# Attention stages: weighted values and row sums from one matrix product, sums merged and inverted on VectorE, another order of the steps

## Chip, cores and metric

The program runs on 1 core of one Trainium2 chip, as a single program of six stages one after the other. The metric is the device time in microseconds of one execution (the median of several). TensorE (PE) multiplies, VectorE (DVE), ScalarE (ACT) and GpSimd (POOL) work on the elements, SyncE (SP) starts most transfers.

## What is computed

A decoder of two layers on x of shape (16, 256, 256): 16 batches of 256 rows with 256 features, all float32. After each part the input is added and every row normalized to mean 0 and variance 1.

- stage "self": causal self-attention with 32 query heads of 16 features and grouped keys and values. Pairs of heads are subtracted with a learned factor (differential attention), and a second product with the output weights follows.
- stage "cross": attention of 16 heads on a context, without a mask, no biases on queries and keys.
- a mixture of experts, and a state-space layer.
- stage "causal": attention of 16 heads on the context with biases and, as the kernel runs it, a causal mask.
- a feed-forward layer with two chosen low-rank experts.

In each attention, for every head:

```python
s = q @ k.T / sqrt(16)            # masked above the diagonal where causal
p = exp(s - max(s))
o = (p @ v) / sum(p)
y = concat(o) @ Wo                # then x + y, normalized by rows
```

## The kernel before

The kernel is written with an explicit program for each engine, and semaphores between them. Each attention stage is one function: `self_attention` for "self", and `cross_attention` for "cross" and "causal". Each has a `body(st)` per engine, run once per step; a step handles several batches at different points of a pipeline. `st.has(d)` asks whether batch (step + d) exists, and `d` = 3 is the batch whose x is being turned and projected, 2 the one whose stacks are loaded from DRAM, 1 the one whose row maxima are computed, 0 and -1 the ones in exponential and weighted sum, -2 the one in the output product (in "self": 0 and -1). Inside a step a loop runs over pairs of heads, 16 in "self" and 8 in the others; here they are called blocks. The order in which the `if i == ...` lines stand in each engine's loop is the order of that engine's queue, and each engine carries it out strictly. The order is written by hand.

In one block PE does, in this order: `scores` of a pair (L1187 in self, L530 in the others) into `score_ps`, of which there is one; `max_scores` of a pair of the next batch (L1168, L509) into one of two `max_ps` banks, with the causal mask added by `mask_half` (L88); in every fourth block `transpose_max` (L1150, L490) of four pairs' maxima; in every odd block `weighted` (L1212, L555); and in most even blocks a projection or output product into the single bank `misc` (L79 to L81, three products of high and low parts for one float32 product).

The values of two heads of a pair lie side by side in `v_pad`, each padded with 16 zero columns, so that a product with 32 columns gives one head's rows of 16 and adds zero to the other's. `weighted` runs four parts: two (`k` = 0, 1) with `v_pad` into the first 256 columns of `out_ps`, and two with the constant `ones` (`lasting_ones`) into the other 256 columns, which so hold the sum of the probabilities, once for each of the 16 feature rows. `par` is the head of the pair; both heads of a tile collect in the same bank. It begins a new tile once `comb_ready` says that ACT's `keep_weighted` (L1293, L647) has copied the bank to `comb`. DVE's `normalize` takes the reciprocal of the sums (L1430, L739) and multiplies (L1434, L743), for each tile. GpSimd's `part_o` splits the result into high and low parts for the output product.

`take_max` on DVE reduces a pair's scores to row maxima: one instruction in cross (L730), two in the causal stages (L1422 and L1423, L726 and L727), because the score blocks of a causal pair lie at columns 0 to 127 and 256 to 511. ACT copies the transposed maxima (`keep_max`), and one block later its `load_row` writes them by DMA into a row of the query stack (L1266, L630), for which `scores` of that tile waits. Other steps that the change touches: `transpose_x` and the split of x into `x_hi` (ACT) and `x_lo` (DVE, L778) in block 5 of cross and causal; `norm_rows` in block 3, which adds the residual and takes the moments; in self `sort_k` (POOL, L1532) in block 15, `sort_q` of tile 0 (ACT, L1276) in block 14, `output_1` of 24 products in block 14, `pad_v` in block 10.

## Time and profile before

| | |
|---|---|
| median of 3 runs | 2752.08 us (2749.12 to 2754.55) |
| profiled execution, its own time | 2760.98 us |
| its span | 2759.3 us |
| PE / DVE / POOL / ACT busy | 88% / 70% / 56% / 52% of the span |
| instructions | 67851 |
| stage self, first to last scores | 66.6 to 688 us |
| stage cross | 753 to 1079 us |
| stage causal | 2177 to 2490 us |

The busy shares are means over six stages that have different limits, so the windows of single batches are of more use than the page's total. In a timeline a line gives the start in us, the duration in us, the engine, the line of the kernel, the instruction and its tiles, and a count where equal instructions were merged. Records of PE overlap, since matmuls are pipelined: what counts is the distance of the starts.

### The profile page before, as it was taken

The page shows a single profiled execution, that of the slowest core. Times are in us where ns is not written, and L with a number is a line of the kernel's source. Part 1 is how long each engine was busy: PE and PEld are TensorE (multiplying, and loading weights), DVE is VectorE, ACT ScalarE, POOL GpSimd, SP SyncE. Part 2 cuts the span into 40 slices and gives each one's busy share as a digit, 9 for nine tenths or more (in the row PEclk, how much of TensorE's full clock was granted, in tenths as well). Part 3 has the DMA queues.
Part 4 walks back from the last instruction along what each step waited for, and adds up shares of the span by engine and source line. Part 5 has one row for each costly group of instructions (what it writes and reads, how often), then busy time and mean ns, then how long its engine had stood idle before and what let it go on. Part 6 is the DMA issues. An engine that isn't in the chain of part 4 may idle for free. (4 is left out here: it accounts for less than half of the span.)

```text
span 2759.3 us, 67851 instructions
## 1 busy us (share of the span) xinstructions
PE 2433.1 (88%) x25528; PEld 2026.7 (73%) x25528; DVE 1932.2 (70%) x3095; ACT 1434.9 (52%) x2255; POOL 1558.9 (56%) x1873
## 2 busy tenths in 40 slices
PE   5999999998699996998999994888896799997998
PEld 4677667766566764988999993677775577765998
DVE  2677667777377876344888885999985377775776
ACT  2566556655256664323665663656563355553333
POOL 3666566665344542055666665777755477763433
PEclk9899999999699998899999997999997899998999
DMA  8555556651677772024666663111001877851111
GB/s 201 129 148 151 131 145 152 146 131 37 180 185 195 198 202 72 16 96 149 220 229 221 216 217 118 37 41 47 22 13 31 238 192 210 214 140 35 58 57 50
DMA packets 228043, 363.58 MB, mean 132 GB/s; under 512 B 52720, under 2 KB 157168, under 8 KB 220272
## 3 DMA queue, kind: packets, MB, share of 16 engines
q1 hardware_dynamic: 207248, 281.31, 38.8%
q0 software_dynamic: 17376, 78.13, 8.1%
q8 instruction: 157, 2.57, 0.4%
q10 hardware_dynamic: 3200, 1.05, 0.2%
q14 instruction: 62, 0.51, 0.1%
HBM read 231.72 MB, written 133.69 MB: 132 GB/s over the span
## 5 line engine op out<-in xcount | busy, mean ns | idle before, releaser
L1285 ACT ACTIVATE self_probs<-self_score_ps 128x768 f32<-128x768 f32 x256 | 208.1, 813 | 201.2 <-PE self_score_ps L1187 199.2
L1501 POOL TENSOR_SCALAR_AFFINE_SELECT self_probs<-self_probs 128x512 f32<-128x512 f32 x256 | 167.3, 655 | 199.1 <-ACT self_probs L1285 198.7
L1422 DVE TENSOR_REDUCE self_neg_max<-self_max_ps 128x2 f32<-128x256 f32 x256 | 107.9, 422 | 204.0 <-PE self_max_ps L88 203.8
L730 DVE TENSOR_REDUCE cross_neg_max<-cross_max_ps 128x4 f32<-128x1024 f32 x128 | 156.0, 1222 | 77.6 <-PE cross_max_ps L509 76.6
L640 ACT ACTIVATE cross_probs<-cross_score_ps 128x1024 f32<-128x1024 f32 x128 | 131.1, 1024 | 96.7 <-PE cross_score_ps L530 96.5
L1423 DVE TENSOR_REDUCE self_neg_max<-self_max_ps 128x2 f32<-128x512 f32 x256 | 174.2, 681 | 0.0
L2213 POOL TENSOR_TENSOR moee_h_lo<-moee_h,moee_h_hi 128x512 fp32r<-128x512 f32 x78 | 112.0, 1437 | 92.9 <-ACT moee_h_hi L1950 92.1
L1950 ACT ACTIVATE moee_h_hi<-moee_h 128x512 fp32r<-128x512 f32 x110 | 69.5, 632 | 182.0 <-DVE moee_h L2116 152.4
L3508 POOL TENSOR_TENSOR ffn_g_lo<-ffn_g_full,ffn_g_hi 128x512 fp32r<-128x512 f32 x64 | 82.2, 1284 | 129.0 <-ACT ffn_g_hi L3394 116.7
L640 ACT ACTIVATE causal_probs<-causal_score_ps 128x768 f32<-128x768 f32 x128 | 103.8, 811 | 95.4 <-PE causal_score_ps L530 95.3
L1187 PE MATMUL self_score_ps<-self_q_stack,self_k_stack 49*128 49x128 f32 (+1 forms) x1024 | 131.3, 335 | 24.4 <-ACT self_probs L1285 10.7
L2116 DVE TENSOR_TENSOR moee_h<-moee_u_ps,moee_silu 128x512 f32<-128x512 f32 x110 | 75.5, 686 | 98.0 <-PE moee_u_ps L81 43.6
L79 PE MATMUL moee_g_ps<-moee_x_hi,moee_in_hi 128*128 128x256 f32 x440 | 131.9, 300 | 12.9 <-DVE moee_x_lo L2103 6.9
L1187 PEld LDWEIGHTS self_score_ps<-self_q_stack,self_k_stack 49*128 49x128 f32 x1024 | 78.9, 191 | 70.9 <-issue 39.0
L1168 PE MATMUL self_max_ps<-self_k_stack,self_q_stack 48*128 48x128 f32 (+1 forms) x1024 | 108.6, 291 | 24.4 <-POOL self_k_stack L1532 22.5
L2156 POOL DMA_INDIRECT x_tiles<-kept_x,moek_slot x64 | 65.8, 1028 | 113.8 <-issue 101.0
L79 PE MATMUL moee_u_ps<-moee_x_hi,moee_in_hi 128*128 128x256 f32 x440 | 126.3, 287 | 3.5 <-issue 3.3
L81 PE MATMUL moee_g_ps<-moee_x_hi,moee_in_lo 128*128 128x256 f32 x440 | 126.2, 287 | 2.2 <-issue 2.1
L823 POOL TENSOR_SCALAR_AFFINE_SELECT causal_probs<-causal_probs 128x512 f32<-128x512 f32 x128 | 84.2, 658 | 77.0 <-ACT causal_probs L640 74.0
L80 PE MATMUL moee_u_ps<-moee_x_lo,moee_in_hi 128*128 128x256 f32 x440 | 125.6, 285 | 1.8 <-issue 1.8
L79 PE MATMUL moee_y_ps<-moee_out_hi,moee_h_hi 128*128 128x256 f32 x440 | 125.1, 284 | 1.5 <-DVE moee_out_lo L2068 1.5
L80 PE MATMUL moee_g_ps<-moee_x_lo,moee_in_hi 128*128 128x256 f32 x440 | 125.7, 286 | 0.5 <-issue 0.5
(500 smaller groups left out, 9668.0 us busy)
## 6 DMA issues: line engine op xcount, KB each, us to landing
self_q<-self_q_split SPq DMA_DIRECT2D x48, 512.0 KB, 3.4
self_q_raw<-self_q SPq DMA_DIRECT2D x32, 768.0 KB, 8.0
cross_stacks<-cross_qk SPq DMA_DIRECT2D x64, 384.0 KB, 6.5
causal_stacks<-causal_qk SPq DMA_DIRECT2D x64, 384.0 KB, 6.6
moe_y_tiles<-lasting_y_out SPq DMA_DIRECT2D x55, 256.0 KB
mid<-lasting_y_out SPq DMA_DIRECT2D x48, 256.0 KB, 2.2
x_tiles<-zeros SPq DMA_DIRECT2D x16, 624.0 KB, 5.2
moee_xT<-x_tiles SPq DMA_DIRECT2D x39, 256.0 KB
```

The lines of the kernel that those rows point to most:

```text
L79: pe.matmul(out, a[0], b[0], start=start, stop=False, **kw)
L80: pe.matmul(out, a[0], b[1], start=False, stop=False, **kw)
L81: return pe.matmul(out, a[1], b[0], start=False, stop=stop, **kw)
L640: nc.scalar.activation(probs[i // 2][:, a, :, lo:], score_ps[:, :, lo:], ACT.Exp, scale=HD ** -0.5).then_inc(prob_ready, 1)
L730: last = dve.tensor_reduce(neg_max[p][:, tile, :, col % 4, :], bank[:].rearrange("p a (q k) -> p a q k", q=QT), AX.X, ALU.max, negate=True)
L1168: last = pe.matmul(max_ps[i % 2][:, ab, q * S:q * S + (q + 1) * P], q_stack[rows, 4 * tile + c, q * P:(q + 1) * P], k_stack[p][rows, tile, ...
L1187: last = pe.matmul(score_ps[:, ab, j * S + k * P:(j + 1) * S], k_stack[p][rows, tile, k * P:(k + 1) * P], q_stack[rows, 4 * tile + c, k * P:],
L1285: nc.scalar.activation(probs[g % 4][:, a, :, P:], score_ps[:, :, P:], ACT.Exp, scale=HD ** -0.5).then_inc(prob_ready, 1)
L1422: dve.tensor_reduce(neg_max[:, tile, :, c, 0:1], bank[:, :, 0:P], AX.X, ALU.max, negate=True)
L1423: dve.tensor_reduce(neg_max[:, tile, :, c, 1:2], bank[:, :, S:2 * S], AX.X, ALU.max, negate=True).then_inc(max_kept, 1)
L1501: pool.affine_select(diagonal, diagonal, [[0, 2], [0, 2], [1, P]], ALU.is_ge, zero, base=0, channel_multiplier=-1).then_inc(prob_masked, 1)
L2213: pool.tensor_tensor(h_lo[p][f][:].rearrange("p j s -> p (j s)"), h[f][:], h_hi[p][f][:].bitcast(F32).rearrange("p j s -> p (j s)"), ALU.s ...
```

## The change

- `weighted` runs two parts in place of four. The 16 columns beside a head's values in `v_pad` hold zeros but for one column of ones (column `tile` and every second one after it), set once at the start of a stage. Each head of the pair now has its own half of `out_ps` (columns `par * S` on), so that a half holds in 16 rows the values of one head and in the other 16 rows its sums.
- The two heads' halves are brought together in two steps: ACT's `cross_weighted` copies `out_ps` with the halves exchanged and one kind of row set to zero (`halves[:, 1:2]` as scale) to `crossed`, and DVE's `merge` adds `out_ps` times the other mask. `weighted` of the next tile waits for `merged_ready`.
- The sums of two tiles stand in alternating rows, so `add_sums` adds the two tiles' sum planes (on GpSimd in cross and causal, on DVE in self), `invert` takes one reciprocal for both, and `normalize` spreads it to the rows with `stream_shuffle` and multiplies.
- `take_max` of the causal stages reads three blocks of 128 columns that now lie side by side, with one reduction into `block_max`; `join_max` takes the smaller of two negated maxima for four pairs at once, and `transpose_max` waits for `max_joined`.
- In cross and causal x is turned in block 7 for the batch 4 ahead, in place of block 5 for the batch 3 ahead; `project_v` of the next block 0 waits for `xlo_ready`. `finish_rows` is in two halves, and the residual is added ahead of the reduction of block 3.
- In self `output_1` runs as two halves in blocks 12 and 14, `sort_k` is in block 11, `sort_q` on ACT in four halves, `pad_v` in block 14; `v_nat` is loaded behind the queries and waits for `v_padded`.
- `load_row` follows `keep_max` in the same block, and `cross_weighted` stands ahead of the exponential.

The core of the diff, for `cross_attention`; `self_attention` has the same steps with its own block numbers:

```diff
@@ weighted
                 if par == 0 and (tile or st.has(d - 1)):
-                    pe.wait_ge(comb_ready, st.at(d) * 2 + tile)
-                for part in range(4):
-                    k = part % 2
-
+                    pe.wait_ge(merged_ready, st.at(d) * 2 + tile)
+                for k in range(QT):
                     first_q = P if causal and k == 1 else 0
                     cols = slice((1 - k) * S + first_q, (2 - k) * S)
                     for quad in range(4):
                         rows = slice(32 * quad, 32 * quad + 32)
-                        if part < 2:
-                            lhs = v_pad[p][:, k, tile * 4 + quad, par, :, :].rearrange("p a e -> p (a e)")
-                            out0 = 0
-                        else:
-                            lhs, out0 = ones[:, par, :], S
-                        last = pe.matmul(out_ps[rows, out0 + first_q:out0 + S], lhs,
+                        lhs = v_pad[p][:, k, tile * 4 + quad, par, :, :].rearrange("p a e -> p (a e)")
+                        last = pe.matmul(out_ps[rows, par * S + first_q:(par + 1) * S], lhs,
                                          probs[g][:, quad % 2, quad // 2, cols],
-                                         start=(par == 0 and part == 0),
-                                         stop=(par == 1 and part == 3), skip_group_check=True)
+                                         start=k == 0, stop=k == QT - 1, skip_group_check=True)
@@ ACT
-            def keep_weighted(st, d, tile):
+            def cross_weighted(st, d, tile):
                 act.wait_ge(pv_done, st.at(d) * 4 + 2 * tile + 2)
                 if st.has(d - 1):
-                    act.wait_ge(o_ready, st.at(d) * 2 + tile - 1)
-                nc.scalar.activation(comb[tile][:].rearrange("p a s -> p (a s)"), out_ps[:],
-                                     ACT.Identity).then_inc(comb_ready, 1)
+                    act.wait_ge(merged_ready, st.at(d) * 2 + tile - 1)
+                nc.scalar.activation(crossed[tile][:, ::-1, :], out_ps[:].rearrange("p (a s) -> p a s", s=S),
+                                     ACT.Identity, scale=halves[:, 1:2]).then_inc(crossed_ready, 1)
@@ DVE
+            def join_max(st, tile):
+                dve.wait_ge(max_kept, st.at(1) * PAIRS + 4 * tile + 4)
...
+                dve.tensor_tensor(neg_max[st.parity(1)][:, tile], block_max[:, :, :, 0:2], block_max[:, :, :, 0::2],
+                                  ALU.min).then_inc(max_joined, 1)
+
+            def merge(st, d, tile):
+
+                dve.wait_ge(crossed_ready, st.at(d) * 2 + tile + 1)
...
+                dve.scalar_tensor_tensor(merged[tile][:], out_ps[:].rearrange("p (a s) -> p a s", s=S),
+                                         halves[:, 0:1], crossed[tile][:], ALU.mult, ALU.add).then_inc(merged_ready, 1)
+
+            def invert(st, d):
+                dve.wait_ge(sums_ready, st.done(d))
+                dve.reciprocal(inv_sum, sums).then_inc(inv_ready, 1)
+
             def normalize(st, d, tile):
 
                 n = st.at(d) * 2 + tile
-                dve.wait_ge(comb_ready, n + 1)
-                dve.reciprocal(inv_sum[:, tile, :], comb[tile][:, 1, :]).then_inc(inv_ready, 1)
-                dve.wait_ge(inv_ready, n + 1)
+                dve.wait_ge(inv_ready, st.done(d))
+                if tile or st.has(d - 1):
+                    dve.wait_ge(o_ready, n)
+                dve.memset(gate[:], 0.0)
+                dve.stream_shuffle(scale[:], inv_sum, [HD + tile] * HD + [tile] * HD).then_inc(scale_ready, 1)
+                dve.wait_ge(scale_ready, n + 1)
@@ DVE, self, body
                 for i in range(PAIRS):
                     if st.has(1):
                         take_max(st, i)
+                    if i == 11 and st.has(0):
+                        normalize(st, 0, 3)
+                    if i % 4 == 3 and st.has(1):
+                        join_max(st, i // 4)
                     if i == 1 and st.has(3) and st.has(2):
                         lower_x(st)
+                    if i in (2, 6, 10) and st.has(0):
+                        merge(st, 0, i // 4 + 1)
+                    if i in (2, 10) and st.has(0):
+                        add_sums(st, 0, i // 8)
                     if i == 3 and st.has(-1):
                         norm_rows(st)
+                    if i in (4, 10) and st.has(0):
+                        invert(st, 0, i // 8)
+                    if i in (5, 6) and st.has(0):
+                        normalize(st, 0, i - 5)
                     if i == 5 and st.has(-1):
                         shift_rows(st)
-                    if i in (3, 7, 11) and st.has(0):
-                        normalize(st, 0, i // 4 + 1)
+                    if i == 10 and st.has(0):
+                        normalize(st, 0, 2)
+                    if i == 14 and st.has(1):
+                        merge(st, 1, 0)
```

## Rows read from the trace of the kernel before

**Rows 1.** The page, part 1: busy time, share of the span, instructions.

```profile
PE 2433.1 (88%) x25528; PEld 2026.7 (73%) x25528; DVE 1932.2 (70%) x3095; ACT 1434.9 (52%) x2255; POOL 1558.9 (56%) x1873
```

**Rows 2.** Windows of one batch each (self, cross, causal): busy us by engine, clock, DMA share.

```profile
306.20:344.50 38.30, 36.48 (x537) 27.73 (x534) 28.20 (x51) 24.23 (x38) 25.46 (x33) 1.00 0.62 149
881.00:901.90 20.90, 20.06 (x249) 14.47 (x248) 16.55 (x22) 13.44 (x21) 10.54 (x16) 1.00 0.81 203
2309.37:2329.65 20.28, 19.72 (x282) 15.15 (x280) 15.26 (x32) 12.19 (x23) 15.45 (x23) 1.00 0.80 206
```

**Rows 3.** Waits of PE, self, cross, causal: us in total, times, longest.

```profile
PE self_max_ps L1168 <- POOL self_k_stack L1532: 15.7, 11, 1.5
PE self_score_ps L1187 <- ACT self_probs L1285: 10.7, 27, 0.9
PE cross_score_ps L530 <- DMA cross_stacks<-cross_max_row: 9.3, 11, 2.1
PE causal_score_ps L530 <- DMA causal_stacks<-causal_max_row: 10.0, 14, 1.4
```

**Rows 4.** Timeline of PE, self: start us, us, instruction.

```profile
303.93 0.86 PE L1212 MATMUL self_out_ps<-self_probs,self_v_pad 128*32 128x256 f32 x16
304.61 0.83 PE L1212 MATMUL self_out_ps<-self_probs,lasting_ones 128*32 128x256 f32 x16
305.37 0.50 PE L1187 MATMUL self_score_ps<-self_q_stack,self_k_stack 49*128 49x128 f32 x4
```

**Rows 5.** Timeline of PE, cross.

```profile
883.31 1.07 PE L555 MATMUL cross_out_ps<-cross_probs,cross_v_pad 128*32 128x256 f32 x16
884.20 1.05 PE L555 MATMUL cross_out_ps<-cross_probs,lasting_ones 128*32 128x256 f32 x16
```

**Rows 6.** Groups of DVE instructions: count, busy us, mean ns, idle before.

```profile
L1422 DVE TENSOR_REDUCE self_neg_max<-self_max_ps 128x2 f32<-128x256 f32 x256 | 107.9, 422 | 204.0 <-PE self_max_ps L88 203.8
L1423 DVE TENSOR_REDUCE self_neg_max<-self_max_ps 128x2 f32<-128x512 f32 x256 | 174.2, 681 | 0.0
L730 DVE TENSOR_REDUCE cross_neg_max<-cross_max_ps 128x4 f32<-128x1024 f32 x128 | 156.0, 1222 | 77.6 <-PE cross_max_ps L509 76.6
L1430 DVE RECIPROCAL self_inv_sum<-self_comb 128x256 f32<-128x256 f32 x64 | 111.6, 1744 | 2.1 <-ACT self_comb L1293 2.1
L1434 DVE TENSOR_TENSOR self_o_full<-self_comb,self_inv_sum 128x256 f32<-128x256 f32 x64 | 36.0, 562 | 2.9
L2809 DVE SCALAR_TENSOR_TENSOR ssm_xs<-ssm_in_ps,ssm_cw,ssm_xs 128x510 f32<-128x510 f32 (+2 forms) x96 | 71.1, 744 | 3.6 <-ACT ssm_xs L2605 1.3
```

**Rows 7.** Timeline of PE and DVE in self: starts of four blocks, normalization of rows.

```profile
309.41 0.51 PE L1187 MATMUL self_score_ps<-self_q_stack,self_k_stack 49*128 49x128 f32 x4
314.02 0.49 PE L1187 MATMUL self_score_ps<-self_q_stack,self_k_stack 49*128 49x128 f32 x4
331.93 0.50 PE L1187 MATMUL self_score_ps<-self_q_stack,self_k_stack 49*128 49x128 f32 x4
341.39 0.50 PE L1187 MATMUL self_score_ps<-self_q_stack,self_k_stack 49*128 49x128 f32 x4
...
333.82 0.68 DVE L1444 TENSOR_TENSOR self_r<-self_misc,self_x_res 128x512 f32<-128x512 f32 x1
335.71 1.75 DVE L1430 RECIPROCAL self_inv_sum<-self_comb 128x256 f32<-128x256 f32 x1
```

**Rows 8.** Timeline of PE, cross: transpose of the maxima, scores that need their row.

```profile
881.01 0.28 PE L490 MATMUL cross_max_ps<-lasting_ident,cross_neg_max 128*16 128x128 f32 x1
...
890.79 0.51 PE L530 MATMUL cross_score_ps<-cross_stacks 49*128 49x256 f32 x4 [0.73 <-DMA cross_stacks<-cross_max_row]
```

**Rows 9.** PE's long idle time in self, and windows with a lower clock.

```profile
284.10 0.50 PE L1187 MATMUL self_score_ps<-self_q_stack,self_k_stack 49*128 49x128 f32 x4 [3.55 <-issue]
...
284.00:291.00 7.00, 6.90 (x63) 4.38 (x65) 2.64 (x5) 2.48 (x4) 4.30 (x5) 0.56 0.38 76
200.00:210.00 10.00, 8.52 (x117) 5.67 (x117) 6.63 (x10) 3.70 (x7) 6.82 (x7) 0.83 0.52 87
```

More of the change, by code:

```diff
@@ L141, in __init__ @@
         self.mask = m.sb("mask", [P, 2, P], BF16)
-        self.ones = m.sb("ones", [P, 2, 32])
+        self.halves = m.sb("halves", [P, 2])
         self.y_out = [m.sb(f"y_out{i}", [P, QT, D]) for i in range(2)]
@@ L150, in load_constants @@
         sp.dma_start(self.mask[:], self.a["mask"]).then_inc(loaded, 16)
-        sp.dma_start(self.ones[:], self.a["ones"]).then_inc(loaded, 16)
+        sp.dma_start(self.halves[:], self.a["halves"]).then_inc(loaded, 16)
     def wait_stored(self, eng, stage, count=B):
@@ L665, in body @@
                         keep_max(st, 0, 1)
-                    if i == 1 and st.has(0):
                         load_row(st, 0, 1)
@@ L669, in body @@
                         keep_max(st, 1, 0)
-                    if i == 5 and st.has(1):
                         load_row(st, 1, 0)
@@ L717, in _ @@
             dve.wait_ge(v_zeroed, 2)
+            for t in range(2):
+                for tile in range(2):
+                    for par in range(2):
+                        ones = v_pad[t][:, :, 4 * tile:4 * tile + 4, par, 1 - par, tile::2]
+                        last = dve.memset(ones, 1.0)
+                last.then_inc(v_zeroed, 1)
             def take_max(st, i):
@@ L858, in body @@
                         mask_probs(st, i)
+                    if i == 2 and st.has(-1):
+                        add_sums(st, -1)
                     if i == 0 and st.has(3) and st.has(2):
@@ L1267, in load_row, with sort_q @@
                               max_row[:, tile, :].bitcast(F32)).then_inc(row_loaded[tile][p], 16)
-            def sort_q(st, d, tile):
+            def sort_q(st, d, tile, half):
                 p = st.parity(d)
-                if tile == 0:
+                if tile == 0 and half == 0:
                     act.wait_ge(landed[p], (st.nth(d) + 1) * 4 * 16)
@@ L1327, in body @@
                         keep_max(st, 0, 3)
-                    if i == 1 and st.has(0):
                         load_row(st, 0, 3)
@@ L1414, in _ @@
                 dve.memset(v_pad[t][:], 0.0).then_inc(v_zeroed, 1)
+            dve.wait_ge(v_zeroed, 2)
+            for t in range(2):
+                by_tile = v_pad[t][:].rearrange("p (j u k) a b e -> p j u k a b e", u=2, k=QT)
+                for tile in range(2):
+                    for par in range(2):
+                        last = dve.memset(by_tile[:, :, tile, :, par, 1 - par, tile::2], 1.0)
+                last.then_inc(v_zeroed, 1)
             def take_max(st, i):
@@ new lines, in merge @@
+            def merge(st, d, tile):
+                n, b = st.at(d) * TILES + tile, tile % 2
+                dve.wait_ge(crossed_ready, n + 1)
+                if tile >= 2 or st.has(d - 1):
+                    dve.wait_ge(sums_ready, st.at(d) * 2 + tile // 2)
+                    dve.wait_ge(o_ready, n - 1)
+                dve.scalar_tensor_tensor(merged[b][:], out_ps[:].rearrange("p (a s) -> p a s", s=S),
+                                         halves[:, 0:1], crossed[b][:], ALU.mult, ALU.add).then_inc(merged_ready, 1)
@@ L1426, in normalize, with add_sums, invert @@
+            def add_sums(st, d, half):
+                n = st.at(d) * 2 + half
+                dve.wait_ge(merged_ready, 2 * n + 2)
+                dve.tensor_tensor(sums, merged[0][:, 1, :], merged[1][:, 1, :], ALU.add).then_inc(sums_ready, 1)
+            def invert(st, d, half):
+                dve.wait_ge(sums_ready, st.at(d) * 2 + half + 1)
+                dve.reciprocal(inv_sum, sums).then_inc(inv_ready, 1)
             def normalize(st, d, tile):
                 n, b = st.at(d) * TILES + tile, tile % 2
-                dve.wait_ge(comb_ready, n + 1)
@@ L1430, in normalize @@
-                dve.reciprocal(inv_sum[:, b, :], comb[b][:, 1, :]).then_inc(inv_ready, 1)
-                dve.wait_ge(inv_ready, n + 1)
+                dve.wait_ge(inv_ready, st.at(d) * 2 + tile // 2 + 1)
+                if tile or st.has(d - 1):
+                    dve.wait_ge(o_ready, n)
+                dve.memset(gate[:], 0.0)
+                dve.stream_shuffle(scale[:], inv_sum, [HD + b] * HD + [b] * HD).then_inc(scale_ready, 1)
+                dve.wait_ge(scale_ready, n + 1)
                 if tile >= 2 or st.has(d - 1):
@@ L1477, in body @@
                                           ALU.subtract).then_inc(ylo_ready, 1)
-                    if i == 15 and st.has(1):
-                        normalize(st, 1, 0)
             run(dve, body)
```

294 lines of the change are left out of this document (176 added, 118 removed).

## The prediction

> **What bounds the kernel now.** I read the page's busy shares first: TensorE (PE) is busy for 88% of the span [rows 1]. That average covers six stages, and the change edits three of them, so I then cut one whole batch out of each, with its own window [rows 2]. A batch of self-attention takes 38.3 us and PE is busy for 36.5 of them, a batch of cross 20.9 with 20.1, a batch of causal 20.3 with 19.7; DVE comes next with 28.2, 16.6 and 15.3. Here the reader sees that PE is the bound in all three, and also how near the second engine is: in cross DVE is only 3.5 us behind. Third, who PE waited for [rows 3]: in self 15.7 us in 11 waits for the sorted keys of GpSimd, in cross 9.3 and in causal 10.0 us for the DMA that puts the maxima into the stacks; DVE is in none of these groups. Each attention runs 16 batches.
>
> **What is removed on PE.** `weighted` multiplies each pair of probabilities twice, once with the values and once with `lasting_ones`, 16 matmul records each [rows 4]. The ones are now columns of `v_pad`, so the second half is gone. From start to start the value half takes 0.68 us in self, the ones half 0.76, in which the change of tile shape at its end is counted [rows 4]; that change stays, so I take 0.68 for what goes. Causal has the same shapes, cross takes all 256 columns in both products: 0.89 us [rows 5]. Eight calls per self batch give 5.44 us, four per cross batch 3.56, four per causal batch 2.72. Moving `sort_k` from step 15 to step 11 (its data and `score_done` of the old batch are both there by step 8) takes away the wait of about 1.46 us per self batch [rows 3]. The halved output product is the same 24 products in two blocks; before, block 12 had no product behind its maxima and PE waited there for the exponential (10.7 us in 27 waits, 0.7 per batch [rows 3]), which the first half now covers; I take 0.5. PE alone would give 38.3 - 5.44 - 1.46 - 0.5 = 30.9, 20.5 - 3.56 = 17.0 and 20.3 - 2.72 = 17.6 us per batch, in all (7.4 + 3.5 + 2.7) x 16 = 218 us. (For cross I use 20.5, the mean of its batches, of which the window cuts one of the longest.)
>
> **What is added on DVE.** Maxima: one reduction of 768 elements in place of one of 256 (422 ns) and one of 512 (681). It lies between the 681 of 512 and the 1222 of 1024 elements, so about 950 ns; it is followed after 0.88 us, since the next instruction starts some 0.08 us before the end, and saves 0.15 us a pair. `join_max` works on 16 elements, 0.06 to 0.2 us, I take 0.12. The reciprocal at 1744 ns is paid once for two tiles: minus 3.5 us per self batch, minus 1.74 per cross or causal batch [rows 6]. `merge` reads 512 elements of PSUM and 512 of SBUF: nearest is the 744 ns of the state-space stage's SCALAR_TENSOR_TENSOR from PSUM, bounds 0.6 to 0.8, I take 0.72 a tile. `stream_shuffle` is in no row; an instruction on 256 elements takes at least the 0.42 of the short reduction and at most the 0.68 of the long one, and I take 0.42, 0.35 to the next; with gate, semaphore and multiply (L1434, 562 ns) `normalize` becomes 1.0 us. The Trainium skill, page "VectorE: DVE Perf Modes", section "The perf-mode tier table", gives a shuffle of 2048 elements about 2400 ns, whatever the permutation; by it 256 elements would be an estimated 0.35 us, so near the lower bound, and no run here shows it yet. `add_sums` is 0.4 us twice on DVE in self, and on GpSimd in the others, whose batches have room (POOL 10.5 of 20.9, 15.5 of 20.3 [rows 2]); it costs something only where GpSimd is late. DVE's sum hardly moves: 28.2 stays near 28, 16.6 becomes 17.1, 15.3 becomes 14.8. So the gain of PE brings DVE level with it in cross and close in self, and what is late next is decided by the order on DVE.
>
> **Walk through the order.** PE's `max_scores(i)` may be two pairs ahead of DVE, but `transpose_max` waits for all of DVE's reductions and now for `join_max`, and every second `weighted` waits for `merge`, which waits for ACT's copy and stands behind DVE's queue (before, that copy alone freed the bank). Self, block 3 to 7: PE needs 341.39 - 331.93 = 9.46 us [rows 7], less two halves of 0.68, 8.1. DVE has four reductions 3.5, join 0.1, residual and moments 1.9 (333.82 to 335.71 in the same group), invert 1.8, one normalize 1.0, shift 0.3, merge 0.7: 9.3. Merge comes some 1.3 us late, and join 1 of block 8 another 0.4. Block 10 to 12: PE needs 4.61 - 0.68 = 3.9 us [rows 7]; between the same points DVE has two reductions 1.75, merge 0.7, sums 0.4, invert 1.8, two normalizes 2.0, join 0.1 = 6.75, so the transpose in block 12 waits 2.9 us. With 0.2 for `y_lo` the batch takes 30.9 + 4.8 = 35.7; gain 2.6 x 16 = 42 us. Cross: from the output product's end in block 2 to the `weighted` of block 7 PE has four blocks, half a batch of 20.5 less two halves of 0.89, and 0.6 of scores and maxima, 9.1 us; DVE has residual 0.6, four reductions at 1.15 (1222 ns less the overlap) 4.6, moments 1.3, invert 1.8, shift 0.3, normalize 1.0, merge 0.7, with 0.3 to start 10.6: merge is 1.5 us late. Then a normalize 1.0, a reduction 1.15 and, new there, `lower_x` 0.65, for which `project_v` of the next block 0 now waits: 2.8 against 1.65 of PE, 1.15 late. PE's own work is 17.0 less the 0.6 per batch of DMA waits [rows 3], 16.4; with 2.65 and 0.2 for the DMA of the maxima the batch takes 19.2; gain 1.3 x 16 = 21 us. Causal: by the same steps with reductions at 0.88 and two joins, DVE has 9.7 against 9.6 of PE, then 2.6 against 1.65: 17.6 - 0.6 + 1.1 + 0.3 = 18.4; gain 1.9 x 16 = 30 us. Everything the walk gives is priced from the rows above; a waiting product or transpose on PE holds back the scores behind it, and through them ACT and GpSimd, but not DVE.
>
> **Moves that I price at little.** `cross_weighted` is the same ACT copy as before, now ahead of the exponential of its block: the exponential is up to 0.8 us later, hidden behind the 12 projection products of every even block. `load_row` goes one block earlier, so its two DMAs no longer stand behind an exponential: today the transpose is issued at 881.01 and the scores that need the row go on at 890.79 [rows 8]; the issue comes 1 to 1.3 us earlier, but four blocks of PE are now only about 8 us, so the same DMA wait remains (0.2 to 0.3 taken; 0 to 1.2). SP's `v_nat` load stands behind the query loads and a wait for `pad_v`; behind it only the zero fill and the store are queued. The 8 small memsets of ones come once per stage before its first maxima, 0 to 2 us per stage. In `sort_q` two halves replace one ACTIVATE, at some 0.1 us more.
>
> **The clock.** After PE's idle 3.55 us the granted clock is 0.56 over 7 us, so for nearly 6 of them at the level of 1.2 GHz; in a stretch of 10 us in which PE was idle for only 1.5 us (busy 8.52) it is 0.83, so it fell as well [rows 9]. The first costs 2.5 to 3 us on top of the wait, the second 1.7. The waits of 2.9 and 1.3 us that I expect in self are of that kind; I count a quarter of a fall more per batch than today, 1.7 x 0.25 x 16 = 7 us. The Trainium skill, page "TensorE: Matmul & The Clock Gate", section "Why this matters for your kernels", warns of gaps between bursts for the same reason; by this rule, which the rows bear out, each batch would fall, and that is the third rival.
>
> **The sum**: 42 + 21 + 30 + 2 for the shorter drains (0 to 5) - 7 = 88. The profiled execution took 2760.98 us for a span of 2759.3, against the median 2752.08; the profile is 0.3% slow, and I take the difference off the median: 2664 us.
>
> **The rivals.** (1) PE alone sets the time: DVE's backlog is absorbed in its two pairs of lead, or the shuffle and merge are shorter. For it: DVE's sum is below PE's in two stages. Against it: the 6.75 against 3.9 us of block 10. All of it gives 2752 - 218 = 2534, half of the late waits gone 2590. Chance 0.2. (2) My forecast, PE and DVE in turn, 2664: 0.5. (3) The late waits lower the clock in every self batch (1.7 to 2.5 us x 16, 27 to 40 us), or DMA takes over: its share of 0.81 at 20.9 us is 0.88 at 19.2 with the same bytes. Both lead to 2685 to 2715. Chance 0.2. (4) Slower: the same mechanism in all stages. If the clock falls twice per self batch (5 us) and once in the others (2.5), the batches are 40.7, 21.7 and 20.9: 38 + 19 + 10 = 67 us slower, 2819. It decides from the point where the falls cost more than the gain, that is 2.6 us per self batch, 5.2 us at the lower level. Chance 0.05. (5) About no change, as a mixture of both near 2752: 0.05. That the products would not disappear can be excluded by the diff.
>
> **Range and chances.** Eight in ten: 2575 to 2710, which leaves out the full form of rival 1 and the slow end. The likeliest case's own range is 2625 to 2695 (shuffle and merge at either bound change four tiles per self batch by 0.4 us each at most). A measurement of this kernel can tell about 0.2% from no change. Faster by more: 0.90; within: 0.03; slower: 0.07.
>
> **What would show it.** No matmul of `lasting_ones`; 16 records per `weighted` and a score 0.76 us after its start in self. No PE wait for `self_k_stack`. Reductions of 768 at 0.95 us, shuffles near 0.4, merges near 0.72. New waits of PE: `transpose_max` for `join_max` (about 3 us in block 12 of self), `weighted` for `merge`, `project_v` for `lower_x`. Batches of 35.7, 19.2 and 18.4 us. The forecast is wrong if PE's idle time does not grow (rival 1), if a steady self batch no longer has the clock of 1.00 of [rows 2] (rival 3), or if DMA waits of the rows are the longest of PE.

## The result, and the profile after

The changed kernel takes 2769.22 us (median of 5 runs, 2765.64 to 2775.84) against 2749.12 us (2743.95 to 2754.55) for the kernel before on the same chip: a ratio of 1.0083, interval 1.0067 to 1.0098. It is slower, by 0.8%, where 2664 us was forecast; the measured time lies outside the range of 2575 to 2710 us too.

The page of the profile after, beside [rows 1]: span and busy times.

```profile
span 2767.5 us, 60507 instructions
PE 2339.3 (85%) x21432; PEld 1958.8 (71%) x21432; DVE 1993.1 (72%) x3311; ACT 1449.9 (52%) x2287; POOL 1576.6 (57%) x1905
```

The three changed stages, each from its first to its last scores; first the kernel before, then the changed one (self, cross, causal in either). Columns as in [rows 2]: window, length, busy us of PE, PEld, DVE, ACT and POOL, clock, DMA share, GB/s.

```profile
66.64:687.91 621.27, 581.91 (x8255) 434.00 (x8255) 434.14 (x768) 369.96 (x561) 390.74 (x510) 0.96 0.55 131
753.21:1078.58 325.37, 305.18 (x3717) 216.10 (x3716) 245.65 (x306) 202.61 (x297) 149.11 (x217) 0.97 0.71 178
2176.94:2489.45 312.51, 295.38 (x4195) 224.00 (x4195) 223.55 (x425) 181.09 (x321) 225.31 (x341) 0.99 0.72 187
```

```profile
64.37:726.89 662.52, 556.38 (x6239) 413.41 (x6239) 480.90 (x827) 381.78 (x591) 385.75 (x506) 0.85 0.53 123
793.84:1100.57 306.73, 263.06 (x2719) 188.68 (x2719) 246.23 (x410) 203.03 (x297) 157.19 (x230) 0.95 0.74 190
2194.31:2495.36 301.05, 267.78 (x3201) 201.09 (x3200) 233.35 (x442) 183.20 (x323) 235.97 (x354) 0.95 0.73 193
```

Cross is 18.6 us shorter and causal 11.5; self is 41.2 us longer, though PE has 2016 matmul records fewer in it. In self PE's busy time fell by only 25.5 us and its idle time (length of the stage less busy time) rose by 66.8, from 39.4 to 106.1 us. What it waited for in self (us in total, times, longest), to be set beside [rows 3]:

```profile
PE self_max_ps L1228 <- DVE self_neg_max L1506: 73.8, 28, 5.6
PE self_score_ps L1265 <- issue: 9.4, 3, 3.4
PE self_out_ps L1284 <- DVE self_merged L1516: 8.5, 14, 1.8
```

The wait for `self_k_stack` is gone as forecast. A new one of 73.8 us stands in its place: the transpose of the maxima (L1228) waits for `join_max` (L1506), for 4.9 us in block 12 of nearly every batch; the other times among the 28 are waits of 0.3 to 0.5 us in block 8. One wait of 4.9 us, on three engines. DVE's chain in blocks 10 and 11 (start us, us, instruction):

```profile
322.11 0.96 DVE L1498 TENSOR_REDUCE self_block_max<-self_max_ps 128x6 f32<-128x768 f32 x1 [0.67 <-PE self_max_ps L88]
322.99 0.74 DVE L1516 SCALAR_TENSOR_TENSOR self_merged<-self_out_ps,lasting_halves,self_crossed 128x512 f32<-128x512 f32 x1
323.76 1.19 DVE L1522 TENSOR_TENSOR self_merged<-self_merged 128x256 f32<-128x256 f32 x1
324.99 1.75 DVE L1526 RECIPROCAL self_merged<-self_merged 128x256 f32<-128x256 f32 x1
327.26 1.63 DVE L1539 TENSOR_TENSOR self_o_full<-self_merged,self_scale 128x256 f32<-128x256 f32 x1
328.82 0.94 DVE L1498 TENSOR_REDUCE self_block_max<-self_max_ps 128x6 f32<-128x768 f32 x1
330.17 0.66 DVE L1539 TENSOR_TENSOR self_o_full<-self_merged,self_scale 128x256 f32<-128x256 f32 x1
330.75 0.16 DVE L1506 TENSOR_TENSOR self_neg_max<-self_block_max 128x16 f32<-128x16 f32 x1
```

GpSimd's two sorting copies beside it, and PE, which stood:

```profile
322.66 2.02 POOL L1657 CAST self_q_stack<-self_q_raw 128x1024 fp32r<-128x1024 f32 x1
326.69 1.92 POOL L1648 CAST self_k_stack<-self_k_raw 128x1024 fp32r<-128x1024 f32 x1
```

```profile
325.73 0.34 PE L88 MATMUL self_max_ps<-lasting_mask,lasting_identb 64*128 64x256 bf16 x4
330.97 0.38 PE L1228 MATMUL self_max_ps<-lasting_ident,self_neg_max 128*16 128x128 f32 x1 [4.90 <-DVE self_neg_max L1506]
```

Two things are to be seen. The sum (L1522) takes 1.19 us, where it takes 0.43 with no copy beside it, and the multiply (L1539) 1.63 in place of 0.42; each ends 0.27 to 0.28 us behind the end of a copy, the sum behind that of Q and the first multiply behind that of K. The second multiply takes 0.66 us; no sorting copy runs beside it, but GpSimd's `part_o` of the tile before (L1629, 329.82 to 330.55) does. The merge, which reads PSUM and SBUF, and the shuffle, which reads one buffer of SBUF, keep their durations beside these copies (0.74 and 0.44 us). From the start of the first reduction to the end of the join DVE takes 8.8 us; with the three operations at their undisturbed times it would be 6.6.

The Trainium skill, page "SBUF — State Buffer", section "Terms", says that VectorE and GpSimd arbitrate for one pair of ports and that the loser blocks for the whole instruction; the trace agrees in that the sum and the multiply end only behind the copy beside them.

The second thing is behind the wait. The same place in an earlier batch, in windows of 2 us:

```profile
158.73:160.73 2.00, 0.00 (x1) 0.00 (x1) 1.91 (x6) 0.00 (x0) 1.50 (x3) 0.57 0.97 271
160.73:162.73 2.00, 2.00 (x10) 2.00 (x11) 0.96 (x1) 0.93 (x2) 1.12 (x2) 0.50 0.89 263
162.73:164.73 2.00, 2.00 (x15) 1.68 (x16) 0.00 (x0) 0.68 (x2) 0.00 (x0) 0.50 0.24 86
164.73:166.73 2.00, 2.00 (x30) 1.12 (x28) 0.96 (x1) 1.91 (x3) 0.64 (x1) 0.72 0.00 0
166.73:168.73 2.00, 2.00 (x24) 1.67 (x20) 1.53 (x2) 1.06 (x2) 0.78 (x2) 1.00 0.00 0
```

The clock has the two levels 1.00 (2.4 GHz) and 0.50 (1.2 GHz), so a mean c over a stretch means a share 2(1 - c) of it at the low one: here 1.7 + 2 + 2 + 1.1 = 6.8 us, of which some 5 fall on PE's work behind the wait. Over the stage the mean of 0.85 means 199 us at the low level, against 50 us before at 0.96.

Not all of it lies behind the waits of block 12. The first batch of the stage and the last two, in the kernel before:

```profile
66.64:107.47 40.83, 37.78 (x466) 27.20 (x467) 22.91 (x38) 22.30 (x33) 22.48 (x28) 0.79 0.53 124
619.70:687.91 68.21, 61.14 (x919) 43.08 (x919) 48.70 (x88) 37.68 (x56) 39.94 (x58) 0.97 0.12 38
```

The same in the changed kernel:

```profile
64.37:106.90 42.53, 41.50 (x354) 29.29 (x354) 23.38 (x33) 23.15 (x35) 18.66 (x24) 0.57 0.56 129
646.10:726.89 80.79, 65.50 (x679) 44.87 (x675) 57.52 (x108) 41.22 (x60) 40.19 (x58) 0.74 0.18 44
```

The first batch has 37 us at the low level in place of 17, the last two 42 in place of 4. The thirteen batches between them have 119 us in place of 31.

### The profile page after: what moved, and what is told of

It is laid out like the page before. It is cut to its first block and busy times, and to the rows that moved or that the text cites. A ratio compares the mean times of both kernels' runs of the same rounds, so it can differ in the third digit from the quotient of the medians.

```text
span 2767.5 us, 60507 instructions
## 1 busy us (share of the span) xinstructions
PE 2339.3 (85%) x21432; PEld 1958.8 (71%) x21432; DVE 1993.1 (72%) x3311; ACT 1449.9 (52%) x2287; POOL 1576.6 (57%) x1905
## 5 line engine op out<-in xcount | busy, mean ns | idle before, releaser
L1498 DVE TENSOR_REDUCE self_block_max<-self_max_ps 128x6 f32<-128x768 f32 x256 | 243.5, 952 | 197.9 <-PE self_max_ps L88 195.7
L1265 PE MATMUL self_score_ps<-self_q_stack,self_k_stack 49*128 49x128 f32 (+1 forms) x1024 | 141.6, 359 | 27.4 <-issue 9.4
L741 DVE TENSOR_REDUCE causal_block_max<-causal_max_ps 128x6 f32<-128x768 f32 x128 | 121.4, 949 | 60.0 <-PE causal_max_ps L88 58.8
L1265 PEld LDWEIGHTS self_score_ps<-self_q_stack,self_k_stack 49*128 49x128 f32 x1024 | 86.0, 208 | 79.7 <-issue 36.2
L1284 PE MATMUL self_out_ps<-self_probs,self_v_pad 128*32 128x256 f32 (+1 forms) x2048 | 125.1, 368 | 9.4 <-DVE self_merged L1516 8.5
L81 PE MATMUL moee_u_ps<-moee_x_hi,moee_in_lo 128*128 128x256 f32 x440 | 125.8, 286 | 0.0
```

Source lines behind the costliest of these rows:

```text
L81: return pe.matmul(out, a[1], b[0], start=False, stop=stop, **kw)
L741: last = dve.tensor_reduce(block_max[:, :, col % 4, :], bank[:, :, 0:3 * P].rearrange("p a (j t) -> p a j t", t=P), AX.X, ALU.max, negate= ...
L1265: last = pe.matmul(score_ps[:, ab, j * S + k * P:(j + 1) * S], k_stack[p][rows, tile, k * P:(k + 1) * P], q_stack[rows, 4 * tile + c, k * P:],
L1284: last = pe.matmul(out_ps[rows, par * S + first_q:(par + 1) * S], lhs, probs[g % 4][:, quad % 2, quad // 2, cols], start=k == 0, stop=k == ...
L1498: dve.tensor_reduce(block_max[:, :, c, :], max_ps[i % 2][:, :, 0:3 * P].rearrange("p a (j t) -> p a j t", t=P), AX.X, ALU.max, negate=True ...
```

## The experiments

Theory A was: the loss lies wholly in self; DVE's chain makes the wait in block 12, and the clock falls because PE stood. The rivals: the clock falls since PE has less to do, wherever the wait lies (B); the wait only changes its place (C); GpSimd's copies make the whole of what the wait exceeds the forecast by (D). All times are medians beside runs of the kernel before on the same chip. The runs fall into three groups on three chips, with 2747.15 us for the kernel before in the first (`cross_new`, `self_new`, `join_first`, `sortk13`), 2749.42 in the second (`join_mid`, `spread`, `spread_k12`, `cross_exp_first`) and 2756.86 in the third (`join_late`, `join_first_k12`, `join_first_k15`), so kernels of different groups are to be compared by their ratios.

**Where the loss lies.** Two mixtures: the changed `cross_attention` (both stages) with the `self_attention` of before, and the reverse.

```
cross_new:  cross_attention of the changed kernel, self_attention of the kernel before
self_new:   self_attention of the changed kernel, cross_attention of the kernel before
```

> The changed cross and causal stages with the self stage of before. Theory A (the loss lies wholly in the self stage, by the wait ahead of block 12's transpose and the clock behind it): the cross stage is 19 us shorter than before, the causal stage 11 us, the self stage as before (622 us, clock 0.96), total 2719 us (2712 to 2728). Rival B (stages with less PE work draw a lower clock wherever they stand, and the two stages profiled shorter only by chance of one execution): 2735 to 2750 us.

> The changed self stage with the cross and causal stages of before. Theory A: the self stage takes 663 us at a clock of 0.85 as in the changed kernel, the others as before, total 2790 us (2780 to 2800). Rival B (the three stages' losses and gains are spread otherwise, part of the loss comes from the boundaries): 2765 to 2780 us.

Measured: 2716.07 us (ratio 0.989, 0.9871 to 0.9909) and 2773.85 us (1.0095, 1.0078 to 1.0112). The windows of `cross_new` for cross and causal:

```profile
744.58:1048.55 303.97, 259.94 (x2719) 186.49 (x2719) 245.56 (x409) 202.82 (x296) 156.35 (x229) 0.96 0.75 192
2139.20:2440.32 301.12, 271.54 (x3201) 202.63 (x3200) 234.84 (x442) 183.95 (x323) 235.12 (x354) 0.94 0.74 195
```

The new cross and causal stages alone gain 31 us, as expected, and this run's rival B (2735 us or more) is out. The new self stage alone loses 27; 2773.85 is below theory A's 2780 to 2800 and inside the 2765 to 2780 of that run's rival. So the loss is in self, but the sizes do not add up: -31 and +27 make 4 us less than before, and both parts together measured 20 more. Part of the 24 us lies in stages that no edit touches: from cross's last to causal's first scores the same code took 1098.4 us before, 1093.7 in the changed kernel, 1090.7 in `cross_new` and 1083.4 in `self_new`. I have no cause for that, and read from here on the self stage itself beside the totals.

**The order of DVE in block 11.** The chain ahead of the join is made shorter in three steps.

```diff
 join_first
     if i % 4 == 3 and st.has(1):
         join_max(st, i // 4)
+    if i == 11 and st.has(0):
+        invert(st, 0, 1)
+        normalize(st, 0, 2)
+        normalize(st, 0, 3)
```

(with the same three calls deleted from ahead of it; in `join_mid` `invert` stays ahead, in `join_late` `invert` and `normalize(st, 0, 2)`.)

> The changed kernel with one order changed in the self stage on VectorE: in block 11 the joined maxima come ahead of the reciprocal and of both normalizations. Theory A (the 4.9 us wait of block 12's transpose is VectorE's chain in front of it, and the clock falls only because PE stood for it): that wait falls below 0.5 us, a wait of 1 to 2.5 us appears at block 14's products of maxima (for the reduction behind the chain), the clock of the stage rises from 0.85 to 0.92 or more, a batch takes 36 to 38 us, total 2700 to 2725 us. Rival B (the clock falls because PE has less to do, wherever the wait stands): the clock stays near 0.85 and the total at 2735 to 2750 us. Rival C (the wait merely changes its place in full): 2765 us.

> The changed kernel with the joined maxima of block 11 ahead of both normalizations, but behind the reciprocal (1.75 us): one step between the changed kernel and the run in which the join comes ahead of the reciprocal too. Theory A (the wait of block 12 is VectorE's chain, operation for operation): the wait is 1.5 to 2.2 us, where it was 4.9 us in the changed kernel and 0.3 us in the other run. For the clock this tells two cases apart: a wait of this length lowers the clock in every batch: self stage 620 to 640 us, total 2730 to 2745 us; it does not: self stage 605 to 615 us, total 2710 to 2722 us.

> The changed kernel with only the last normalization of block 11 behind the joined maxima; sum, reciprocal and the other normalization stay ahead. Theory A (one operation less in the chain, one duration less in the wait; the clock goes by the length of the wait): the wait is 3.2 to 3.9 us, between 2.6 us (join ahead of both normalizations, 2719 us) and 4.9 us (2769 us); the clock is at its low level for 3 to 7 us behind it in each batch, total 2738 to 2756 us. If total time doesn't go by this wait: 2765 us or more.

Measured: 2698.13 us (0.9809, 0.9792 to 0.9825), 2719.49 (0.9883, 0.986 to 0.9906) and 2759.88 (1.0014, 0.9999 to 1.003). PE's waits in self with the join first:

```profile
PE self_max_ps L1246 <- DVE self_block_max L1498: 13.1, 14, 1.0
PE self_out_ps L1284 <- DVE self_merged L1516: 8.2, 14, 1.8
PE self_max_ps L1228 <- DVE self_neg_max L1506: 7.5, 25, 0.8
```

One batch of the changed kernel, and one of `join_first`:

```profile
160.73:200.92 40.19, 34.04 (x406) 25.75 (x407) 31.23 (x54) 24.91 (x39) 25.40 (x33) 0.92 0.58 142
```

```profile
226.79:261.62 34.83, 32.21 (x408) 24.09 (x408) 30.00 (x55) 24.38 (x39) 25.37 (x33) 1.00 0.72 166
```

The same instructions, 5.4 us apart: 3.5 of idle time, 1.8 of PE time through the clock. The wait of block 12 went from 4.9 us to 0.2, and only 1.0 us came back at block 14, where the products of the maxima wait for the reduction behind the chain. The self stage went from 662.5 to 591.1 us. The total is 2 us below the range of theory A, and the batch 1 us shorter than it said. Rival C is out, and so is B for the steady batches: PE has the same work, and a steady batch has a clock of 1.00. The stage's clock is 0.90, not 0.92, which means some 115 us at the low level. 31 of them lie behind the three stops of 2.8 to 2.9 us in which nothing that the profile shows is waited for ("issue"): the clock is low for 10.2 us behind each, where in the kernel before it was low for 3.4 to 6.8. Most of the rest lies in the first batch and the last two:

```profile
64.50:106.30 41.80, 40.80 (x356) 28.67 (x356) 23.41 (x33) 23.19 (x35) 18.72 (x24) 0.58 0.54 129
584.40:655.80 71.40, 62.21 (x667) 42.60 (x667) 55.70 (x108) 39.00 (x57) 39.90 (x57) 0.78 0.17 46
```

That is 35 and 31 us at the low level, nearly as much as in the changed kernel, so the wait of block 12 does not make it. What does was not tested, and for these three batches rival B is not excluded.

Between the two, `join_mid` waits 2.6 us (1.5 to 2.2 expected) and `join_late` 3.96 (3.2 to 3.9); `join_late`'s 2759.88 us lies 4 above its range of 2738 to 2756, on the chip on which the kernel before was slowest. `join_mid`'s median lies where I expected it if the clock did not fall. Its trace shows at least 3.4 us at the low level in 11 of the 13 middle batches, but it is the trace of the slowest of its five executions (2732.93 us), so how often the clock falls in the others is not shown.

**GpSimd's copy.** `sort_k` at block 13 in place of 11, DVE as in the changed kernel.

```diff
-                    if i == 11 and st.has(2):
+                    if i == 13 and st.has(2):
                         sort_k(st)
```

> The changed kernel with GpSimd's sorting copy of K in the self stage in block 13 in place of 11; VectorE's order is untouched. Theory A (VectorE's own chain of merge, sum, reciprocal, two normalizations, reduction and join makes most of the 4.9 us, the copy stretches one multiply in it from 0.42 to 1.63 us): the wait falls to 3.7 us, total 2745 to 2755 us. Rival D (GpSimd's copies make the whole difference between 4.9 us and the chain's 2.9 us, and both VectorE operations recover): the wait falls to 2.9 us, 2725 to 2740 us. If the stretched operations have nothing to do with the copy: 2769 us.

Measured: 2742.63 us (0.9988, 0.9968 to 1.0009), self stage 627.0 us. The time lies under theory A's 2745 to 2755 us and above rival D's 2725 to 2740. The same two operations of DVE, one batch:

```profile
224.90 1.80 DVE L1522 TENSOR_TENSOR self_merged<-self_merged 128x256 f32<-128x256 f32 x1
229.00 0.42 DVE L1539 TENSOR_TENSOR self_o_full<-self_merged,self_scale 128x256 f32<-128x256 f32 x1
```

```profile
223.80 2.03 POOL L1657 CAST self_q_stack<-self_q_raw 128x1024 fp32r<-128x1024 f32 x1
225.76 0.65 POOL L1618 TENSOR_SCALAR_AFFINE_SELECT self_probs<-self_probs 128x512 f32<-128x512 f32 x1
```

With the copy gone both multiplies of this batch are back at 0.42, while the sum, still beside the copy of Q and the mask behind it, takes 1.80. The wait fell to 3.5 us in most batches (4.0 in some, beside such a sum), not to D's 2.9. So the K copy's stretching is shown, and it is the smaller part of the wait. But 1.4 us less of waiting, 22 us in 16 batches, came with 35 us less in the stage. The low clock behind the wait lasted 3.4 us in most batches, where it had been 6.8. 4 us of the 35 lie in the stage's first batch, which has 25 us at the low level in place of 37; why is not known.

**The chain laid out over more blocks.**

```
spread
 DVE:  block 11: join_max, add_sums(1), invert(1); block 12: normalize(2); block 13: normalize(3)
 POOL: part_o(2) in block 13, part_o(3) in block 14
 PE:   output_1(st, 1) in block 15, ahead of weighted; ACT's y_hi in block 15
spread_k12: as spread, and sort_k in block 12 in place of 11
```

> The changed kernel with VectorE's chain of block 10 and 11 in the self stage laid out over four blocks: join first, then sum and reciprocal in block 11, normalizations in blocks 12 and 13, the lower parts in 13 and 14, the second half of the output product in block 15 ahead of the weighted product. Theory A (VectorE's order alone makes the waits): the waits of block 12 (4.9 us) and of block 14 (1.0 us with the join first) are both under 0.4 us, a batch takes 33.8 to 34.8 us, total 2680 to 2692 us. Rival C (the wait changes its place to block 15 or to the transposes of x, 1 us or more): 2696 to 2710 us.

> As the run before it, with GpSimd's sorting copy of K in block 12 in place of 11. If the copy costs by what runs beside it on VectorE (sum and multiply between SBUF buffers are stretched, reductions from PSUM are not): within 5 us of the run before it, since one multiply is stretched in either. If its place matters as in the changed kernel (27 us for two blocks): 15 us or more apart.

Measured: 2745.17 us (0.9975, 0.9953 to 0.9997) and 2725.72 us (0.9918, 0.9889 to 0.9947). Both theory A's 2680 to 2692 us and rival C's 2696 to 2710 are missed, by 35 us and more. Of rival C the mechanism holds: the waits change their place. PE's waits in `spread`, and its clock around one pair of them:

```profile
PE self_score_ps L1265 <- ACT self_probs L1359: 21.0, 30, 1.4
PE self_misc L79 <- POOL self_o_lo L1632: 16.1, 13, 1.4
```

```profile
238.00:240.00 2.00, 0.86 (x12) 0.60 (x12) 2.00 (x4) 0.81 (x1) 1.92 (x5) 1.00 0.80 233
240.00:244.00 4.00, 3.82 (x28) 3.03 (x28) 1.68 (x3) 0.60 (x1) 1.31 (x4) 0.57 0.18 37
```

The waits are now 1.4 us of the scores for ACT, which sorts Q and copies the product in the same blocks, and 1.3 us for `o_lo`, 2.2 us apart; the clock falls for 3.4 us behind them in every batch. Steady batches are 37.2 to 37.7 us in both kernels. The 19 us between them, against my expectation of 5, lie in the traces in self (14 us, in the first, third, twelfth and thirteenth batch) and in causal (7 us), whose code is the same (305.1 and 297.6 us). I leave that open.

**The join first, with the K copy elsewhere.** `sort_k` in block 12, and in block 15 as before the change.

```diff
-                    if i == 11 and st.has(2):
+                    if i == 12 and st.has(2):
                         sort_k(st)
```

> The version with the join ahead of reciprocal and normalizations (2698 us), with GpSimd's sorting copy of K in block 12 in place of 11. Theory A (a copy costs by the SBUF to SBUF operation of VectorE that runs beside it and by whether that operation is waited for): in block 11 it lies beside the reciprocal, which it doesn't stretch, and one multiply (0.64 us where 0.42 is undisturbed); in block 12 it lies behind them: gain of 0 to 0.3 us for a batch, 2692 to 2699 us. If the place matters as in the changed kernel: 2680 us or less.

> The same version with that copy in block 15, where the kernel before has it. VectorE's chain is undisturbed, but the first products of maxima of the next batch wait for the copy again: 1.5 us (15.7 us in 11 times before), at a place at which nothing else is late. Theory A: total 2712 to 2725 us, self stage 15 to 25 us longer than with the copy in block 11. If the gain of an undisturbed chain outweighs the wait: 2695 us or less.

Measured: 2695.2 us (0.9782, 0.9741 to 0.9822) and 2758.94 us (1.0011, 0.9996 to 1.0026). The first is as expected and the fastest of all, 2.2% under the kernel before. The second was wrong by 35 us. In `join_first_k15`, PE's wait for the keys in self, and windows around one of them and behind it:

```profile
PE self_max_ps L1246 <- POOL self_k_stack L1650: 19.9, 10, 2.3
```

```profile
252.00:254.00 2.00, 0.16 (x2) 0.17 (x3) 0.36 (x1) 0.58 (x1) 2.00 (x2) 0.93 0.00 0
254.00:264.00 10.00, 10.00 (x71) 7.41 (x73) 4.55 (x6) 3.18 (x5) 3.40 (x4) 0.50 0.46 82
```

A wait of 2.2 us, 6 us behind waits of 0.7 and 0.3, is followed by 10.2 us at the low level, in 10 of the 13 middle batches. Such a batch takes 41.3 us, more than a steady one of the changed kernel, though the stage is shorter (644.8 against 662.5 us). So moving `sort_k` ahead of block 15 is right, and with the shorter product it is worth 64 us; in the kernel before, the same copy at the same place cost a wait of 1.46 us [rows 3] and left the clock alone behind 6 of the 11.

**ACT's order in cross and causal.** From `cross_new`, `cross_weighted` behind the exponential of its block.

```diff
+                    if st.has(0):
+                        exponential(st, i)
                     if i == 2 and st.has(-1):
                         cross_weighted(st, -1, 1)
                     if i == 6 and st.has(0):
                         cross_weighted(st, 0, 0)
-                    if st.has(0):
-                        exponential(st, i)
```

> The self stage of before, the changed cross and causal stages, and in these ScalarE's scaled copy of the weighted product behind the exponential of its block in place of ahead of it. Theory E (ScalarE's and VectorE's chain around the weighted product takes what it takes, the scores' waits of 0.5 to 0.8 us only change into waits of the weighted product for the merge): 2712 to 2724 us, against 2716 us with the copy ahead. Rival F (the scores wait only for ScalarE's order): 14 batches of 0.5 to 0.8 us in both stages, 2695 to 2705 us.

Measured: 2731.75 us (0.9929, 0.9905 to 0.9953); cross 307.0 us, causal 300.8, against 304.0 and 301.1. Rival F is out: this order gains nothing. Theory E's 2724 is passed by 8 us, though the two stages together are only 3 us longer than in `cross_new`. The longest waits in cross in `cross_new`:

```profile
PE cross_score_ps L554 <- ACT cross_probs L659: 31.6, 44, 2.7
PE cross_score_ps L554 <- DMA cross_stacks<-cross_max_row: 8.5, 12, 1.9
```

## Why the prediction was wrong

The change was forecast at -88 us and measured at +20. By the traces 76 us of this miss lie in self (621.3 - 42 + 7 = 586 forecast, 662.5 measured), 2 in cross and 18 in causal. Another 12 come from the kernel before, whose profiled execution (2760.98 us) was that much slower than its median.

**The self stage's 76 us** split in three, by the busy and idle times shown above. PE's own work was forecast to fall by 5.44 us a batch, 87 us; from start to start (weighted to next scores 1.44 us, now 0.79) it fell by 0.65 us a call, 83 us: 4 us of the miss. PE's idle time was forecast to grow by (4.8 - 1.46 - 0.5) x 16 = 45 us and grew by 67: 21 us. The rest of the measured +41.2 is -83 + 67 + 58: PE's work took some 58 us more at the lower clock, where 7 were forecast: 51 us. This last term is an estimate, by difference; half of the time at the low level in which PE was busy, counted in windows of half a us, gives 59, and the method is good to some 10 us.

**DVE's prices** were right where they were read alone: reduction 0.95 us (950 forecast), merge 0.74 (0.72), shuffle 0.44 (0.42, bounds 0.42 to 0.68), join 0.16 to 0.32 (0.12), reciprocal once for two tiles. The estimate of 0.35 for the shuffle, from the Trainium skill, page "VectorE: DVE Perf Modes", section "The perf-mode tier table", was 0.1 too low, and plain scaling of that page's figure would even give 0.30.

**The walk through block 10 to 12** named the right place, the right instruction and the right releaser, and gave 2.9 us where 4.9 came: 32 us over 16 batches. PE's side of it was right (3.96 us for 3.9). DVE's chain took 8.8 us for 6.75. The step that failed is "two normalizes 2.0, sums 0.4": these prices leave out what runs beside an operation that reads two SBUF buffers. In the batch shown the sum was stretched by 0.8 us beside GpSimd's copy of Q, the first multiply by 1.2 beside the copy of K, which the change itself had moved there, and the second by 0.2 beside `part_o`. I had priced `sort_k`'s move for the wait that it takes away, not for what it would run next to. The trace of the kernel before held a warning, behind the mean of 562 ns that I used: its multiply takes 0.42 or 0.43 us in 38 of 64 places, 0.55 to 0.77 in 25, and 1.89 in one, where it ends 0.28 us behind the same copy of K.

```profile
88.77 1.98 POOL L1532 CAST self_k_stack<-self_k_raw 128x1024 fp32r<-128x1024 f32 x1
89.14 1.89 DVE L1434 TENSOR_TENSOR self_o_full<-self_comb,self_inv_sum 128x256 f32<-128x256 f32 x1
```

The late merge (1.3) and second join (0.4) were 0.4 each: 14 us given back.

**The clock** is the largest term that failed. I took a quarter of a fall per batch, 7 us, though I had written that waits of 2.9 and 1.3 us are of the kind that lowers it. In the changed kernel it fell in every batch. Of the 148 us more at the low level 89 lie in the thirteen middle batches, and there `join_first` shows the cause: without the wait of block 12 they have 48 us in place of 119. The other 59 lie in the first batch and the last two. No term of the walk had them, `join_first` keeps most of them, and their cause is open. Rival 3 named the fall in every self batch and stopped at 2715, since it let the clock fall on top of waits of the forecast's size. That self takes 591 us with the join first, near the 586 forecast, is partly luck: its steady batches are 0.8 us shorter than forecast, its first and last ones longer.

**Cross and causal.** Cross was forecast at 19.2 us a batch and takes 19.0 to 19.5, but by other waits: not one of merge (0.4 us in all in `cross_new`) or, in steady batches, of `lower_x`, instead the scores' wait for the exponential, 8.5 us before and 31 after. The score bank is single, so the next scores wait for the exponential, and that stands behind other work of ScalarE: in the changed kernel's batch around 907 us three of its operations, of 0.60 to 0.67 us, run between 906.09 us and the exponential's start at 907.72. One order of ScalarE was tried, without a gain, so what would take this wait away is not shown. Causal was forecast at 18.4 and takes 19.0 to 19.1, and the stage gained 11.5 us where 30 were forecast; the wait for the exponential grew there too, from 5.9 to 17.0 us. The clock went from 0.99 to 0.95, from 3.4 to 30 us at the low level, 23 of them in its last two batches. Drains were put down as a gain of 2 us.

**Range and chances.** Slower had 0.07, by clock falls in every batch of all stages; they came in every batch of one, with waits of a size that no rival had. Two bounds belonged into the range: the block-12 wait with each two-buffer operation lengthened by a copy, and a fall behind each wait.

## What to carry over

When work is taken off the bounding engine, list the waits that come in its place by length and by neighbour: here the same wait cost 5 us in the order given and 0.2 with one 16-element operation moved ahead of a reciprocal and two normalizations, 71 us for the self stage. Put what another engine waits for ahead of what none waits for yet, and read a moved operation for what it will run beside, not only for whom it releases. A wait of PE is to be priced with the low clock behind it, by a row of its length (the table below).

## What the runs showed of the hardware

How long the clock stayed low behind PE's waits in steady self batches (worked out from windows as above, of one execution each, while the totals are medians):

| kernel | waits of PE, us | low, us | batch, us | total, us (ratio to before) |
|---|---|---|---|---|
| before | 1.46; 0.36 | 0, in some 3.4 | 38.3 | 2749 |
| join_first | 0.2; 1.0 + 0.3 | 0 | 34.9 | 2698 (0.981) |
| join_first_k12 | 0.7 + 0.3 | 0 | 34.6 | 2695 (0.978) |
| spread | 1.4 + 1.3 | 3.4 | 37.3 to 37.7 | 2745 (0.998) |
| join_mid | 2.6 | 3.4 | 37.2 to 37.5 | 2719 (0.988) |
| sortk13 | 3.5 to 4.0 | 3.4 or 6.8 | 38.0 to 38.7 | 2743 (0.999) |
| join_late | 3.96 | 3.4 or 6.8 | 38.4 to 39.8 | 2760 (1.001) |
| changed kernel | 4.9 | 6.8 in most | 40.2 | 2769 (1.008) |
| join_first_k15 | 0.7 + 0.3, then 2.2 | 10.2 | 41.3 | 2759 (1.001) |

Not expected: two waits of 1.4 and 1.3 us lower the clock as a single one of 2.6 does, and the longest low time stands behind waits of 3.2 us in all, not behind that of 4.9. The Trainium skill, page "TensorE: Matmul & The Clock Gate", section "HAM oscillation — how this bites in real kernels", tells how waits between short bursts of products bring the clock down again and again. The trace agrees that it falls in every batch, but with gaps of 1.4 and 1.3 us, which are shorter than those of the page's example. Why `join_first_k15` stays low for so long with PE busy in every window is open.

In these traces an operation of DVE that reads two SBUF buffers didn't end while one of GpSimd's sorting copies ran: 0.42 us became 1.63, 1.80 and, in the kernel before, 1.89. The merge (0.74 us, one input in PSUM) beside the copy of Q, and in `join_first` the reciprocal (1.74 us, one buffer) beside that of K, were not lengthened.
